# Decoder layer on one core: a share of the light feed-forward matmuls, the score reads and the heavy layer's loads and turns are moved to other places

## The chip, the cores and the metric

The kernel runs on 1 core of one Trainium2 chip, as one launch. Its metric is the device time of that launch in microseconds (us). TensorE is called PE below, VectorE DVE, ScalarE ACT, GpSimd POOL; SP is the engine that issues most DMAs.

## The reference, cut to what matters

x is (2, 2048, 512) in float32. The layer has three parts, each with a layernorm ahead and a residual sum behind it.

```python
x = x + self_attention(layernorm(x))            # 16 heads of 64, relative position bias
x = x + cross_attention(layernorm(x), context)  # 16 heads of 32, 77 masked keys
x = x + ffn(layernorm(x))
def ffn(x):
    light = gelu(rms_norm(x, gamma_l) @ w1_light + b1_light) @ w2_light + b2_light   # all rows, 256 hidden
    s = x @ routing_token
    a = 0; b = -relu(s)
    for _ in range(50):
        a = eps * log(8) - eps * logsumexp((s + b) / eps);  b = -relu(s + a)
    scores = exp((s + a + b) / eps)
    idx = top_k(scores, 512)                                  # 512 of the 2048 rows of each batch
    heavy = gelu(rms_norm(x[idx], gamma_h) @ w1_heavy + b1_heavy) @ w2_heavy + b2_heavy  # 2048 hidden
    return light + scatter(heavy * gain, idx)
```

## The kernel before, in words

The program has three stages, each in its own block; between two stages all engines meet at a barrier, and the semaphores are cleared. Every matmul that must be exact is done as three products of a high and a low float32r part (hi*hi, hi*lo, lo*hi).

**Stage 1** (`attention`) is the self-attention and takes most of the time. The change does not touch its work.

**Stage 2** (`middle`) walks over 32 tiles of 128 rows (`NTILES = 32`). It is a software pipeline of four ages: in step j, age 0 works on tile j (output projection `wo`, layernorm, turn, query projection), age 1 on tile j-1 (energies and softmax), age 2 on tile j-2 (probabilities turned, values, projection `wo2`, second residual), age 3 on tile j-3 (layernorm, rms norm `r3`, its turn into `t3_hi`/`t3_lo`, dot product with the routing token). In steps 32, 33 and 34 only the older ages are left, so less and less work stands in each. The order on each engine is written out by hand in one `iteration(j, a, here, more)` per engine. SP stores r3, t3 (a high and a low part, 256 KB each per tile), xb (the residual plus bias) and, for each 4 tiles, the scores s into DRAM scratch. At its end SP waits until all stores have landed.

**Stage 3** (`routed`) starts with SP reading the scores back (`s_in`, four small DMAs), the light layer's first weights `wl1` and the normed rows in chunks of 512 tokens (`tokens_in`, two DMAs of 1 MB for each of 8 chunks, into the two halves of `t3`). Then come the 50 routing iterations (`N_ITERS`). Each is one chain: DVE `arg` (L2029), ACT `Exp` (L1936), a PE matmul with one column (L1805), ACT `Ln` (L1939), DVE again. Behind the one-column matmul of each iteration from number 6 on PE gets four of the 192 light-layer matmuls (`hidden_mm`, L1787; one chunk is 24 of them); the 16 that are left stand behind the loop. ACT and DVE split `wl1` into high and low within iterations 3 and 4. A chunk's DMAs are issued when the chunk two before it has been multiplied.

Behind the loop the scores are spread over PSUM (L1817), the 512th largest is searched in five levels on DVE (L2072), and the chosen rows' places are turned to one-hot marks (`hot_of`, L2150) and gathered by matmuls (L1846). In all of these steps light tiles are mixed in: PE `light_mm` (L1800, four passes), then DVE `light_out` (L2022), which needs `xb[j]` from DRAM; SP issues `xb_in(j + 4)` right after it stores tile j. The last 12 tiles (`LIGHT_LAST`, 20 to 31) run beside the marks of batch 1: one mark for each of the first eight, two for each of the last four. SP also loads the heavy layer's `w2` in four DMAs of 1 MB, behind the stores of tiles 8, 12, 16 and 20 (`W2_AT`). ACT makes `w1_hi` (L1957) after the gelus; DVE makes `w1_lo` (`first_weights_low`, L2173), one piece per tile of `LIGHT_LAST`.

Then the gathered rows of batch 0 are turned (`turn_rows`, PE L1882, ACT L1968, DVE `turned_low` L2186), and the heavy layer runs: `first` (L1895) and `second` (L1911), 16 times 12 matmuls each for each of two batches, PE without a gap; last come 8 scatters on POOL.

## Time and profile before

| | us |
|---|---|
| median of 3 runs | 3987.68 (3982.39 to 3989.78) |
| the profiled execution | 3983.49 |
| its span, first to last instruction | 3981.7 |
| PE busy in the span | 3856.2 (97%) |
| end of stage 1, first instructions of stage 2 | about 2990 |
| first instruction of stage 3 | 3610.57 |
| heavy layer's first matmul | 3792.69 |

Times in the rows below are us from the start of the span. A timeline row says when an instruction (or a group of them, xN) starts and how long it takes, and in brackets how long its engine had been idle and what it waited for. "PEclk" is the granted clock of TensorE, 1.00 for 2.4 GHz and 0.50 for 1.2 GHz.

### The profile page before, as it was taken

The page shows a single profiled execution, that of the slowest core. Times are in us where ns is not written, and L with a number is a line of the kernel's source. Part 1 is how long each engine was busy: PE and PEld are TensorE (multiplying, and loading weights), DVE is VectorE, ACT ScalarE, POOL GpSimd, SP SyncE. Part 2 cuts the span into 40 slices and gives each one's busy share as a digit, 9 for nine tenths or more (in the row PEclk, how much of TensorE's full clock was granted, in tenths as well). Part 3 has the DMA queues.
Part 4 walks back from the last instruction along what each step waited for, and adds up shares of the span by engine and source line. Part 5 has one row for each costly group of instructions (what it writes and reads, how often), then busy time and mean ns, then how long its engine had stood idle before and what let it go on. Part 6 is the DMA issues. An engine that isn't in the chain of part 4 may idle for free. (4 is left out here: it accounts for less than half of the span.)

```text
span 3981.7 us, 59812 instructions
## 1 busy us (share of the span) xinstructions
PE 3856.2 (97%) x18973; PEld 2188.4 (55%) x18973; DVE 2459.3 (62%) x3356; ACT 2036.6 (51%) x3452; POOL 2687.4 (67%) x1402
## 2 busy tenths in 40 slices
PE   9999999999999999999999999999998999996899
PEld 7754444444444444444444444444446888884477
DVE  3466666666666666666666666666635777774632
ACT  3335555555555555555555555555543555543232
POOL 1128888888888888888888888888983434330010
PEclk9999999999999999999999999999998999997999
DMA  7642222322223342222322223322312333325710
GB/s 222 170 100 59 59 59 72 99 60 64 60 59 87 88 140 65 59 59 78 94 60 64 60 59 89 82 62 59 99 51 74 107 102 105 101 83 185 282 42 22
DMA packets 395504, 352.29 MB, mean 88 GB/s; under 512 B 193947, under 2 KB 268187, under 8 KB 394008
## 3 DMA queue, kind: packets, MB, share of 16 engines
q1 hardware_dynamic: 327320, 326.04, 28.5%
q10 hardware_dynamic: 66048, 16.78, 1.9%
q0 software_dynamic: 1920, 6.29, 0.5%
q8 instruction: 172, 2.82, 0.3%
q14 instruction: 44, 0.36, 0.0%
HBM read 142.64 MB, written 89.70 MB: 58 GB/s over the span
## 5 line engine op out<-in xcount | busy, mean ns | idle before, releaser
L328 POOL TENSOR_TENSOR acc<-acc,probs 128x1024 f32<-128x1024 f32 x894 | 2128.1, 2380 | 260.5 <-ACT probs L798 135.7
L928 DVE TENSOR_REDUCE maxes<-ps 128x1 f32<-128x1024 f32 x1024 | 1251.2, 1222 | 695.3 <-PE ps L579 690.7
L801 ACT ACTIVATE probs<-ps,far_bias 128x1024 f32<-128x1024 f32 (+7 forms) x1280 | 1023.0, 820 | 1012.2 <-DVE near_s L945 553.8
L614 PE MATMUL ps<-probs,v_head 128*64 128x512 f32 x4096 | 991.8, 605 | 2.0 <-ACT ctx_out L784 2.0
L579 PE MATMUL ps<-stacks 64*128 64x512 f32 x2048 | 747.2, 445 | 16.1 <-issue 7.2
L594 PE MATMUL ps<-stacks 64*128 64x512 f32 x1792 | 659.7, 447 | 0.3 <-ACT probs L798 0.3
L593 PE MATMUL ps<-stacks 128*128 128x512 f32 x2048 | 617.5, 418 | 1.7 <-ACT probs L798 1.7
L594 PEld LDWEIGHTS ps<-stacks 64*128 64x128 f32 x1792 | 275.8, 184 | 501.6 <-issue 329.8
L614 PEld LDWEIGHTS ps<-probs,v_head 128*64 128x64 f32 x4096 | 248.4, 136 | 482.9 <-issue 480.6
L593 PEld LDWEIGHTS ps<-stacks 128*128 128x128 f32 x2048 | 349.7, 188 | 217.8 <-issue 163.6
L945 DVE TENSOR_TENSOR near_s<-ps,near_bias 128x384 f32<-128x384 f32 (+2 forms) x576 | 284.8, 494 | 265.5 <-PE ps L594 243.2
L579 PEld LDWEIGHTS ps<-stacks 64*128 64x128 f32 x2048 | 302.6, 185 | 113.4 <-DVE maxes L928 57.0
L798 ACT ACTIVATE probs<-near_s 128x384 f32<-128x384 f32 (+2 forms) x576 | 271.5, 471 | 0.0
L562 PE MATMUL ps<-xn_hi,w_hi 128*128 128x512 f32 x512 | 203.8, 398 | 0.0
L562 PE MATMUL ps<-xn_hi,w_lo 128*128 128x512 f32 x512 | 203.0, 397 | 0.0
L562 PE MATMUL ps<-xn_lo,w_hi 128*128 128x512 f32 x512 | 202.8, 396 | 0.0
L325 POOL TENSOR_TENSOR acc<-probs 128x1024 f32<-128x1024 f32 x64 | 152.7, 2386 | 38.5 <-issue 31.8
L538 PE MATMUL ps<-stacks,xn_hi 128*128 128x512 f32 x512 | 165.3, 404 | 11.0 <-DVE xn_lo L898 9.0
L1251 POOL TENSOR_TENSOR m_rs<-m_rs,m_expo 128x1 f32<-128x1 f32 x32 | 17.6, 550 | 234.1 <-DVE m_rs L1456 234.1
L1361 PEld LDWEIGHTS m_ps<-m_turned,both_wk 128*128 128x128 f32 x1024 | 122.1, 196 | 4.5 <-ACT m_turned L1419 2.0
L1361 PE MATMUL m_ps<-m_turned,both_wk 128*128 128x128 f32 x1024 | 122.7, 279 | 1.4 <-ACT m_turned L1419 1.4
L1374 ACT COPY m_pt<-m_ps 77x512 f32<-77x512 f32 x128 | 68.4, 583 | 107.5 <-PE m_ps L1282 107.5
(269 smaller groups left out, 4749.3 us busy)
## 6 DMA issues: line engine op xcount, KB each, us to landing
stacks<-c_k SPq DMA_DIRECT2D x128, 256.0 KB, 2.5
stacks<-c_q SPq DMA_DIRECT2D x128, 256.0 KB, 2.6
stacks<-c_d SPq DMA_DIRECT2D x256, 128.0 KB, 2.7
scr_v<-probs ACTq DMA_DIRECT2D x32, 512.0 KB, 4.0
stacks<-c_q SPq DMA_DIRECT2D x128, 128.0 KB, 2.7
v_head<-scr_v SPq DMA_DIRECT2D x32, 512.0 KB, 3.6
scr_ctx<-ctx_out SPq DMA_DIRECT2D x128, 128.0 KB, 2.3
both_ctx<-scr_ctx SPq DMA_DIRECT2D x32, 512.0 KB, 3.9
```

The source lines that it names most:

```text
L328: pool.tensor_tensor(acc[:, qb, :], acc[:, qb, :], pr, ALU.add).then_inc(s["summed"], 1)
L538: mm = pe.matmul(ps[:, value_bank(v), :], xs[i][:, k, t * P:(t + 1) * P], (wv_hi, wv_lo)[j][:, k, half * 512:(half + 1) * 512], start=at = ...
L562: mm = pe.matmul(ps[:, proj_bank(m, tb), :], w[wi][:, kk, :], xs[xi][:, kk, tb * 512:(tb + 1) * 512], start=a == 0, stop=a == len(TERMS) - 1)
L579: mm = pe.matmul(ps[:, max_bank(n, qt, pair) + i, :], stacks[0:64, mside, QA, qt * P:(qt + 1) * P], stacks[0:64, mside, KX, kc * 512:(kc + ...
L593: return pe.matmul(out, stacks[:, side, KA, keys], stacks[:, side, QA, q], start=False, stop=True, skip_group_check=True)
L594: return pe.matmul(out, stacks[64:128, side, KX, keys], stacks[64:128, side, QB, q], start=False, stop=True, skip_group_check=True)
L614: mm = pe.matmul(ps[64 * half:64 * half + 64, PV, :], v_head[:, side, kt, :], probs[:, st % PT_RING, half * 512:(half + 1) * 512], start=k ...
L798: ins = act.activation(probs[:, st % PT_RING, a:z], near_s[:, st % 2, 0:z - a], ACT.Exp)
L801: ins = act.activation(probs[:, st % PT_RING, a:z], sc[:, a:z], ACT.Exp, bias=bias)
L928: dve.tensor_reduce(maxes[:, qt, pair:pair + 1], ps[:, bank:bank + 2, :], AX.XY, ALU.max).then_inc(s["max_done"], 1)
L945: dve.tensor_tensor(near_s[:, st % 2, 0:z - a], sc, near_bias[:, side, j0:j0 + z - a], ALU.add).then_inc(s["biased"], 1)
L1361: mm = pe.matmul(ps[:, Q2, m * P:(m + 1) * P], wq2[:, k, m * P:(m + 1) * P], turned1[:, k, :], start=k == 0, stop=k == KT - 1)
```

## The change

It moves work, and adds no arithmetic.

1. A quarter of the light layer's first matmuls (chunks 0 and 1, 48 of 192) goes into stage 2's last steps: 6 at the head of PE's step 32, 16 at the head of step 33, 14 at the head of step 34 and 12 behind the turns there. SP loads the two chunks (4 DMAs of 1 MB) at the head of its step 32; the very first of the 48 waits for chunk 0. DVE copies the results out of PSUM. `wl1` is loaded at stage 2's start and split at the end of step 30.
2. The scores are read back at the end of stage 2, two DMAs by SP and two by ACT; SP no longer waits there for the last stores, it does so at stage 3's start, ahead of chunks 2 and 3.
3. In the routing loop the light matmuls start in iteration 2, three to an iteration (144 of them), and none stands behind the loop.
4. `w2`'s four loads are issued by ACT, one behind the other, when `w1_hi` is done.
5. The turns of batch 0 (PE, ACT and DVE) go into the last four tiles of `LIGHT_LAST`, in the place of four pieces of `w1_lo`, which are made in the heavy layer's first steps.
6. Buffers are placed anew so that this fits (`keep` and `mask_i` in `e`, `hot` over the old `wl1_hi`/`wl1_lo`, r3's rows of batch 1 over the early hidden values).

```diff
@@ middle: SP @@
+            for dst, name in ((wl1, "w1l"), (gamma_l[:], "gamma_l")):
+                sp.dma_start(dst, io[name]).then_inc(s["wl1_in"], 16)
             def iteration(j, a, here, more):
                 side, other = a % 2, 1 - a % 2
+                if isinstance(j, int) and j == NTILES:
+                    sp.wait_ge(s["wo"], NTILES)
+                    for ch in range(N_EARLY):
+                        for w in range(2):
+                            sp.wait_ge(s["t3_stored"][w], 64 * (ch + 1))
+                        for part in range(2):
+                            sp.dma_start(tokens[ch][:, part, :, :].bitcast(F32),
+                                         scr["t3"][part][:, :, ch * TOKENS:(ch + 1) * TOKENS]).then_inc(s["t3_early"][ch], 16)
...
             iterations(sp, iteration)
-            for side in range(2):
-                sp.wait_ge(s["r3_stored"][side], 16 * NTILES // 2)
-                sp.wait_ge(s["xb_stored"][side], 16 * NTILES // 2)
-                sp.wait_ge(s["t3_stored"][side], 32 * NTILES // 2)
             sp.wait_ge(s["s_stored"], 16 * NBLK)
+            for half in range(2):
+                sp.dma_start(scores_of(NB - 1, half), scr_s[NB - 1, HALF * half:HALF * half + HALF]).then_inc(s["s_in"], 16)
@@ middle: PE @@
+            def light_early(first_at, end_at):
+                for n in range(first_at, end_at):
+                    q, at = divmod(n, len(HIDDEN_TERMS))
+                    ch, m = divmod(q, LM)
+                    if at == 0:
+                        if q == 0:
+                            pe.wait_ge(s["wl1_lo"], 1)
+                            pe.wait_ge(s["x1"], NTILES)
+                        if q == 1:
+                            pe.wait_ge(s["q2"], NTILES * CM)
+                        if m == 0:
+                            pe.wait_ge(s["t3_early"][ch], 32)
+                        if q >= 2:
+                            pe.wait_ge(s["hid"], q - 1)
+                    k, part, w = HIDDEN_TERMS[at]
+                    mm = pe.matmul(ps[:, (WO, Q2)[q % 2], :], (wl1_hi, wl1_lo)[w][:, k, m * P:(m + 1) * P], tokens[ch][:, part, k, :],
+                                   start=at == 0, stop=at == len(HIDDEN_TERMS) - 1)
+                    if at == len(HIDDEN_TERMS) - 1:
+                        mm.then_inc(s["hid_mm"], 1)
             def iteration(j, a, here, more):
+                if isinstance(j, int) and j in EARLY_AT:
+                    light_early(*EARLY_AT[j])
...
                     mm.then_inc(s["rt"], 1)
+                    if isinstance(j, int) and j == NTILES + 2:
+                        light_early(*EARLY_LAST)
@@ middle: ACT, at its end @@
+            act.wait_ge(s["s_stored"], 16 * NBLK)
+            for b in range(NB - 1):
+                for half in range(2):
+                    act.dma_start(scores_of(b, half), scr_s[b, HALF * half:HALF * half + HALF]).then_inc(s["s_in"], 16)
@@ constants @@
-HIDDEN_FROM, HIDDEN_STEP = 6, 4
-SPLIT_AT = 3
+N_EARLY = 2
+EARLY_AT, EARLY_LAST = {NTILES: (0, 6), NTILES + 1: (6, 22), NTILES + 2: (22, 36)}, (36, 48)
+EARLY_OUT = {NTILES + 1: (0,), NTILES + 2: (2, 3)}
+HIDDEN = [(ch, m, at) for ch in range(N_EARLY, NCHUNK) for m in range(LM) for at in range(len(HIDDEN_TERMS))]
+HIDDEN_FROM, HIDDEN_STEP = 2, 3
-G_RING, W2_AT = 3, (8, 12, 16, 20)
+G_RING = 3
+TURN_FROM = len(LIGHT_LAST) - HT
@@ routed: SP @@
-            for b in range(NB):
-                for half in range(2):
-                    s_in(b, half)
-            for dst, name in LOADS_HIDDEN:
-                sp.dma_start(dst, io[name]).then_inc(s["wl1_in"], 16)
-            for ch in range(2):
+            for side in range(2):
+                sp.wait_ge(s["t3_stored"][side], 32 * NTILES // 2)
+                sp.wait_ge(s["xb_stored"][side], 16 * NTILES // 2)
+                sp.wait_ge(s["r3_stored"][side], 16 * NTILES // 2)
+            for ch in range(N_EARLY, N_EARLY + 2):
                 tokens_in(ch)
...
-                if j in W2_AT:
-                    q = W2_AT.index(j)
-                    if q == 0:
-                        sp.wait_ge(s["hidden_mm"], NCHUNK * LM)
-                    sp.dma_start(w2[:, 4 * q:4 * q + 4, :], io["w2h"][:, 4 * q:4 * q + 4, :]).then_inc(s["w2_in"][q], 16)
@@ routed: PE, last light tiles @@
             for i, j in enumerate(LIGHT_LAST):
                 light_mm(j)
                 for t in hots_of(i):
                     hot_mm(1, t)
+                if i >= TURN_FROM:
+                    turn_rows(0, i - TURN_FROM)
@@ routed: ACT, behind w1_hi @@
+            act.wait_ge(s["hidden_mm"], N_HIDDEN_MM)
+            for q in range(4):
+                act.dma_start(w2[:, 4 * q:4 * q + 4, :], io["w2h"][:, 4 * q:4 * q + 4, :]).then_inc(s["w2_in"][q], 16)
@@ routed: DVE, last light tiles @@
                 light_out(j)
-                first_weights_low(i)
+                if i >= TURN_FROM:
+                    turned_low(0, i - TURN_FROM)
+                else:
+                    first_weights_low(i)
             pairs_out(1)
-            turned_low(0)
```

## Rows read from the trace of the kernel before

**Rows 1.** By window: us, busy time by engine, PEclk, DMA share, GB/s.

```profile
3580.00:3600.00 20.00, 9.45 (x69) 7.02 (x67) 11.47 (x20) 6.24 (x10) 3.31 (x6) 0.83 0.26 80
3650.00:3695.00 45.00, 43.18 (x191) 29.57 (x191) 22.86 (x103) 14.99 (x91) 0.00 (x0) 0.97 0.80 264
```

**Rows 2.** Timeline, stage 2's last steps: start, us, engine, line, instruction [idle before].

```profile
3570.80 0.34 SPq L1194 DMA_DIRECT2D scr_xb<-both_wo  x1
...
3572.12 1.10 PE L1282 MATMUL m_ps<-m_ident,m_e 128*77 128x128 f32 x8 [3.07 <-DVE m_e L1518]
...
3587.70 3.76 PE L1282 MATMUL m_ps<-m_ident,m_e 128*77 128x128 f32 x16 [6.72 <-DVE m_e L1518]
...
3603.14 1.12 PE L1335 MATMUL m_ps<-m_ident,m_r 128*128 128x128 f32 x4 [6.18 <-DVE m_r L1483]
...
3606.26 0.64 SPq L1191 DMA_DIRECT2D scr_t<-both_t_lo  x1
```

**Rows 3.** Timeline of stage 3's start.

```profile
3610.58 2.67 SPq L1699 DMA_DIRECT2D r_s_half<-scr_s  x4
...
3614.70 0.18 DVE L1998 TENSOR_REDUCE r_top<-r_s_half 128x1 f32<-128x32 f32 x1 [3.44 <-DMA r_s_half<-scr_s]
...
3617.19 0.24 DVE L2029 TENSOR_SCALAR r_arg<-r_ahead,r_log 128x32 f32<-128x32 f32 x1
...
3618.75 0.24 DVE L2029 TENSOR_SCALAR r_arg<-r_ahead,r_log 128x32 f32<-128x32 f32 x1 [1.31 <-ACT r_log L1939]
```

**Rows 4.** Chain that ended last, in the routing loop: start, us, what.

```profile
3629.28 1.92 PE r_ps L1787 x4
...
3631.41 1.92 PE r_ps L1787 x4
...
3640.11 8.81 DMA r_t<-scr_t
...
3692.52 1.04 PE r_ps L1787 x4
...
3693.88 1.05 PE r_ps L1787 x4
```

**Rows 5.** DMA issues of chunks 0, 1: first; second and third (us to landing).

```profile
r_t<-scr_t SPq DMA_DIRECT2D x1, 1024.0 KB, 7.8
...
r_t<-scr_t SPq DMA_DIRECT2D x2, 1024.0 KB, 11.8
```

**Rows 6.** Timeline behind the routing loop.

```profile
3695.93 0.19 DVE L2060 TENSOR_TENSOR r_score<-r_ex,r_kept 128x32 f32<-128x32 f32 x1
...
3698.76 3.71 PE L1817 MATMUL r_ps<-r_ident,r_score 128*64 128x128 f32 x64
```

**Rows 7.** Timeline: DVE sums of light tiles 20, 24, 25 and 31.

```profile
3759.88 0.69 DVE L2022 TENSOR_TENSOR r_light<-r_ps,r_xb 128x512 f32<-128x512 f32 x1 [0.77 <-PE r_ps L1800]
...
3768.06 0.69 DVE L2022 TENSOR_TENSOR r_light<-r_ps,r_xb 128x512 f32<-128x512 f32 x1 [0.44 <-PE r_ps L1800]
...
3773.22 0.69 DVE L2022 TENSOR_TENSOR r_light<-r_ps,r_xb 128x512 f32<-128x512 f32 x1 [3.41 <-DMA r_xb<-scr_xb]
...
3787.33 0.69 DVE L2022 TENSOR_TENSOR r_light<-r_ps,r_xb 128x512 f32<-128x512 f32 x1
```

**Rows 8.** Chain, heavy layer: its first group, and one further on.

```profile
3792.69 4.57 PE r_ps L1895 x12
...
3803.25 2.72 PE r_ps L1895 x12
```

**Rows 9.** Queues in 3765 to 3767 us: packets, MB, share of 16 engines.

```profile
q1 hardware_dynamic: 101, 0.53, 84.4%
q0 software_dynamic: 27, 0.07, 13.7%
```

**Rows 10.** All DMAs of xb in 3700 to 3790 us.

```profile
DMA to landing us min/median/max: 2.7/3.6/10.2
```

**Rows 11.** Timeline of ACT behind the gelus (w1_hi).

```profile
3707.02 9.91 ACT L1957 ACTIVATE r_w_hi<-r_w,r_gamma 128x512 fp32r<-128x512 f32 x16
```

More of the change, by code:

```diff
@@ L1081, with middle @@
 AGES = 4
-def middle(nc, io, scr, homes):
+def middle(nc, io, scr, homes, early):
     with ExitStack() as c:
@@ L1126, in middle @@
             ctx_hi ctx_lo mask1 zero held held_pool s_stored""".split()}
-        for n in ("ctx_in", "x_in", "xb_stored", "r3_stored", "t3_stored"):
+        for n in ("ctx_in", "x_in"):
             s[n] = (sem(n + "0"), sem(n + "1"))
+        own = dict(s)
+        s.update(early)
         block = c.enter_context(nc.Block())
@@ L1429, in iteration @@
                         act.activation(q2[:, m, :], ps[:, Q2, m * P:(m + 1) * P], ACT.Identity, bias=bq[:, m:m + 1]).then_inc(s["q2"], 1)
+                if isinstance(j, int) and j == NTILES - 2:
+                    act.wait_ge(s["wl1_in"], 32)
+                    for k in range(KT):
+                        ins = act.activation(wl1_hi[:, k, :], wl1[:, k, :], ACT.Identity, scale=gamma_l[:, k:k + 1])
+                    ins.then_inc(s["wl1_hi"], 1)
             context_hi(0, 0)
@@ L1518, in iteration @@
                     dve.tensor_tensor(et, et, sm[:].unsqueeze(2).to_broadcast([P, CH, CL]), ALU.mult).then_inc(s["p"], 1)
+                if isinstance(j, int) and j == NTILES - 2:
+                    dve.wait_ge(s["wl1_hi"], 1)
+                    for k in range(KT):
+                        ins = dve.scalar_tensor_tensor(wl1_lo[:, k, :], wl1[:, k, :], gamma_l[:, k:k + 1], wl1_hi[:, k, :].bitcast(F32), ALU.mult, ALU.subtract)
+                    ins.then_inc(s["wl1_lo"], 1)
+                if isinstance(j, int) and j in EARLY_OUT:
+                    for q in EARLY_OUT[j]:
+                        hidden_out(q)
             iterations(dve, iteration)
-    return all_of(s)
+    return all_of(own)
 HEAVY, NUM_HEAVY = 2048, 512
@@ L1553, in hidden_done @@
     last = len(HIDDEN_TERMS) - 1
-    return [ch * LM + m for ch, m, at in hidden_of(i) if at == last]
+    return [(ch - N_EARLY) * LM + m for ch, m, at in hidden_of(i) if at == last]
 LIGHT_IN_LEVEL = 2
@@ L1581, in hots_of, with routed @@
     return [i] if i < single else [2 * i - single, 2 * i - single + 1]
+N_HIDDEN_MM = (NCHUNK - N_EARLY) * LM
 HALF = P // NB
-def routed(nc, io, scr, out, index):
+def routed(nc, io, scr, out, index, homes, early):
     with ExitStack() as c:
@@ L1661, in routed @@
         HOT, TURN, FIRST, PAIRS = 7, 4, 4, (4, 7)
-        s = {n: sem(n) for n in """weights w1_in const zero s_in s_max_in top_own top_turned top_row top_wide top_mm lift scaled ahead gam dif ex mm logs neg_a neg_mm arg kept sc1 sc score w
+        s = {n: sem(n) for n in """weights w1_in const zero s_max_in top_own top_turned top_row top_wide top_mm lift scaled ahead gam dif ex mm logs neg_a neg_mm arg kept sc1 sc score w
             bc bcr t1 cnt en en_mm f1 f2 base over mm1 r1 r2 r3s sel mm2 p1 p2 place hot hot_mm pairs pairs_tr parts4 gain edge_own edge_mm edge picked index
-            tr trt trl w1_lo w2_hi w2_lo gmm g g_hi g_lo used ymm y1 y scattered light_in wl1_in wl1_hi wl1_lo hidden_mm hidden gelu_l light_mm light""".split()}
+            tr trt trl w1_lo w2_hi w2_lo gmm g g_hi g_lo used ymm y1 y scattered light_in hidden_mm hidden gelu_l light_mm light""".split()}
         for n in ("gathered", "y_in", "t3_in"):
             s[n] = (sem(n + "_0"), sem(n + "_1"))
+        s.update(early)
         for n in ("xb_in", "light_stored", "w2_in"):
@@ L1926, in _ @@
                 if b + 1 < NB:
-                    turn_rows(b + 1)
+                    for t in range(HT):
+                        turn_rows(b + 1, t)
                 second(b, HM - 1)
@@ L1939, in _ @@
                 act.activation(log[:], ps[:, 0, 0:1], ACT.Ln, scale=1.0 / K_ROUTE).then_inc(s["logs"], 1)
-                if i == SPLIT_AT:
-                    act.wait_ge(s["wl1_in"], N_HIDDEN)
-                    for k in range(KT):
-                        ins = act.activation(wl1_hi[:, k, :], wl1[:, k, :], ACT.Identity, scale=gamma_l[:, k:k + 1])
-                    ins.then_inc(s["wl1_hi"], 1)
             act.wait_ge(s["arg"], 1)
@@ L2267, in program, with handed, right @@
         clear(nc, attention(nc, io, scr, homes))
-        clear(nc, middle(nc, io, scr, homes))
-    routed(nc, io, scr, out, index)
+        early = {n: nc.alloc_semaphore("r_" + n) for n in ("s_in", "wl1_in", "wl1_hi", "wl1_lo", "hid_mm", "hid")}
+        for n in ("t3_early", "xb_stored", "r3_stored", "t3_stored"):
+            early[n] = (nc.alloc_semaphore(f"r_{n}_0"), nc.alloc_semaphore(f"r_{n}_1"))
+        clear(nc, middle(nc, io, scr, homes, early))
+    routed(nc, io, scr, out, index, homes, early)
+def handed(nc, c, stage):
+    def right(name, dims, dt=F32):
+        return c.enter_context(nc.sbuf_tensor(stage + name, dims, dt, side="right"))
+    rows_1 = right("rows_1", [P, HT, D])
+    s_half = right("s_half", [P, 2, NT])
+    hidden_0 = rows_1[:, :, :].rearrange("p (m a) d -> p m (a d)", m=LM)
+    return rows_1, s_half, hidden_0, right
 def kernel(**inputs):
```

132 lines of the change are left out of this document (68 added, 64 removed).

## The prediction, made before the run

> **What bounds the kernel now.** I read the busy times by window first: the heavy layer and stages 1 and 2 keep PE full, so only three places are left where moved work can count: stage 2's last steps, where PE works 9.45 us of 20 and the clock is down to 0.83 [rows 1], the routing loop, and the last light tiles with what follows. For each I then read the timeline (what ended the idle time) and the chain that ended last.
>
> In stage 2's last steps each step hangs on the softmax chain of the step before: PE waits 3.07, 6.72 and 6.18 us at the heads of steps 32, 33 and in 34 [rows 2]. The reader should see when SP gets to step 32: its last issue of step 31 starts at 3570.80, because it waits for xb.
>
> Stage 3's start: SP's last issue of stage 2 ends at 3606.90; stage 3 begins at 3610.5; the scores arrive at 3614.7; the routing loop starts at 3617.19 [rows 2, 3]. The first iterations take 1.56 us each, at the low clock [rows 3]. With four light matmuls an iteration takes 2.13 us at 1.2 GHz and 1.36 at 2.4 GHz [rows 4]; in the second, PE is not the bound: it idles 0.37 us of each, waiting for ACT's `Exp`, so 1.35 is the length of the ACT-DVE-PE chain and three matmuls will not shorten it. The whole loop is 76.3 us to the last one-column matmul (3693.50, just ahead of the last row of [rows 4]), against 50 x 1.35 = 67.5; the rest is low clock, the split of `wl1` (1.5) and three waits of 1.1 for chunks that take 9.4 us from issue (0.55 and 8.81 after it, [rows 4]) where PE uses one up in 8.1.
>
> The last light tiles: pace 2.05 us (8.18 for four), then 3.41 us of waiting for xb behind `w2`'s last quarter, and 5.4 us from the last tile's sum to the heavy layer, whose first 12 matmuls take 4.57 us instead of 2.72 [rows 7, 8].
>
> **Stage 2's end.** The 48 matmuls fit into the idle spells, but the first of them waits for chunk 0, and it stands ahead of all of step 32 on PE. SP can issue it only at 3571.15, after xb. When does it land? Two such loads alone took 9.4 us [rows 4]; in stage 3, four in a row landed 7.8, about 10.8, 12.8 and 14.8 us after their own issues, in order, so the second came 11.4 us after the first issue (with 0.5 MB of `wl1` ahead of it) [rows 5]. I take 10.0, so 3581.2. Bounds 9.4 and 11.4. PE then does its six at the low clock (it has idled since 3569; four take 1.92 less overhead, 0.43 each [rows 4]): 2.6 us. The turns of step 32 start at 3583.9 instead of 3572.12: 11.8 late. They and the energies run partly at 1.2 GHz: +1.3 (0.5 to 2.1; the stretch takes 4.1 us at full clock). Behind this everything queues: the energies, DVE's softmax, step 33's turns, SP's stores. Given back: step 33's 16 turns took 3.76 at the low clock; with PE kept busy ahead of them they are ACT-bound, -1.1; step 34's turns 1.12 to 0.66, -0.5. So the tail is 11.5 us late. The 16, 14 and 12 further matmuls (3.8, 3.3, 2.8 us) lie in waits of 6.7 and 6.2 us and beside SP's issues, and cost nothing; if PE were still at 1.2 GHz they would take 6.9, 6.0 and 5.2, and the last would cost about 1.5. The `wl1` split at step 30 (1.7 us on ACT and on DVE) lies under 5.9 us of `wo` matmuls: 0, at most 0.5; the same for its loads at stage 2's start.
>
> SP's two score reads (1.3 us) take the place of the wait for the last stores' landing (2.2), then the barrier (1.4): stage 3 starts at 3606.9 + 11.5 + 1.3 + 1.4 = 3621.1, 10.6 late.
>
> **Routing loop.** The scores are there at 3621.1; DVE's memsets (0.8 us) and 2.5 us of preparation remain: the loop starts at 3624.4, 7.2 late (3.4 won). Iteration 2 then needs chunk 2, issued from 3621.2 on, landed at 3631.2 by the same 10.0; its first light matmul would be ready at 3628.6, so 2.6 us are lost. From there 47 iterations to the last: three at the low clock (2.13 - 0.43 = 1.70), 44 at 1.35, sum 64.5: 3695.7, against 3693.88 [rows 4]: 1.8 late. No chunk is late any more (8 x 1.35 = 10.8 us of use against 9.4 to load). Behind the loop, the scores are ready 2.05 us after this point, but PE begins to spread them only at 3698.76, because of the 16 matmuls in front [rows 6]; now at once: 3697.9. That is 0.8 early. So parts 1 to 3, the bulk of the change, come out at -0.8.
>
> **Level search and w2.** ACT starts the gelus 1.8 late, ends `w1_hi` at 3716.93 + 1.8 = 3718.7 [rows 11], and puts 4 MB on its own queue, in the middle of the search, where SP moves about 235 GB/s of xb and out. xb is asked for four tiles (8.9 us) ahead and takes 3.6 [rows 10], so 5.3 us are spare. How do two queues share? In 3765 to 3767 us SP's queue held `w2`'s quarter (5.2 KB a packet on average, 0.53 MB / 101) and POOL's queue the row gathers (2.6 KB): 84.4% of the DMA time against 13.7% [rows 9]. If xb's queue gets 15 to 20%, `w2` takes some 13 us (3720 to 3733) and SP moves 0.07 MB/us. The pair of tiles 6 and 7 asks at 3721.4 for 1 MB (two stores, two xb); 0.8 is through by 3733, the rest by 3733.7; tile 11 wants its xb at 3728.9: a stall of 4.5 us on DVE, which holds the path. Bounds: 0 if the queues share by need, 9 if the next pair is caught as well. I take 4.5, as the row on sharing is the nearest.
>
> The Trainium skill (DMA: Bandwidth & Descriptors, Queues, rings and completion order) says that each engine goes round between the queues that have work, a whole packet at a time. By that rule 8 KB packets of `w2` against 2 KB ones of xb leave xb a fifth, and the stall is the one above; with equal shares in bytes it would be nothing. The trace's 84.4 to 13.7 agrees with the rule.
>
> **Last light tiles.** Without `w2`'s quarter in front, xb for tile 25 lands some 3 us earlier (1 MB at 340 GB/s), just in time. Tiles 25 to 31 then take 7 x 2.05 plus a second mark's 0.2 in four: 15.0 instead of 19.3, -4.3. The turns make the last four tiles longer: marks 0.9, PE's second mark 0.23 and turn 0.5, ACT's copy 0.6, DVE's low part 0.65 with hand-overs, a ring of 3.1 us in place of 2.2. From the start of these four to the heavy layer: 4 x 3.15 = 12.6 to the last low part, against 4 x 2.18 + 5.4 less the 1.3 in which the last sum stands ahead of its end = about 12.8 before. Hence about 0; with the tighter start -0.2 (bounds -2 and +3: a ring of 2.7 or 4). But PE now idles little before the first group: 4.57 becomes 2.72 [rows 8]: -1.8. The four pieces of `w1_lo` (0.74 each) go under groups of 2.72: 0; first needed at the ninth group, made by the fourth or fifth. The sum of this part: -6.3; from bounds on the stall's return (-3 to -5) and the ring: -3 to -9.
>
> **Sum.** -0.8 + 4.5 - 6.3 = -2.6 us on 3983.49, the profiled execution, which is 4.2 under the median of the runs shown. On the median: 3987.7 - 2.6 = 3985.1.
>
> **Rivals.**
> 1. *The queues share by need*: no stall in the search, -7.1 us, 3980.6. For it: SP's requests are pipelined. Against: the measured shares [rows 9].
> 2. *w2 hits more than one pair of tiles*: 4 to 5 us more, +2, 3990. For it: the stores stand in the same queue. Against: after 3733 the queue drains at some 360 GB/s.
> 3. *The wait for chunk 0 costs little*: if PE got it within the 3.07 us of idle, the tail would be 11.5 us earlier and all of that stays: 3973.6. It decides from a landing at 3572.1 on; the rows give 9.4 us at least from an issue at 3571.15. Very unlikely in full, a part (loads faster with four in flight) less so.
> 4. *Slower: the clock falls in the routing loop.* With three matmuls PE has 0.70 + 0.22 = 0.92 us of work in 1.35, and idles 0.4 to 0.6 in each iteration; with four the clock was 0.97 over the loop [rows 1]. If it stays at 1.2 GHz, 44 iterations of 1.70 add 15.4 us: 4000.5. It is slower by over 0.2% from about 30 such iterations on. Against it: in the one-hot stretch (3740 to 3756) PE has 2.4 of 3.7 us and keeps the full clock.
>
> The Trainium skill (TensorE: Matmul & The Clock Gate, A second HAM failure mode: psum-queue depth-cycling) tells of a kernel in which frequent short idle spells between groups of matmuls made the clock swing between its levels. By that rule the loop comes out as rival 4 has it; the loop with four, at 0.97, neither shows nor excludes it.
>
> **How the numbers follow.** My forecast (stall of one pair, full clock) 0.48; rival 1 0.22; rival 2 0.12; rival 3, in full or half, 0.10; rival 4, in full or half, 0.08. The range for 8 in 10 takes in rivals 1 and 2, the landing bounds (±1.5 twice), the clock's 2 us and the turns' +3: 3975 to 3995. 0.2% is 8 us, about what a measurement of this kernel can tell from no change. Faster by more: rival 3, 0.08; a third of rival 1 with its errors, 0.08; 0.05 of the main case: 0.21. Slower by more: rival 4, 0.07; a third of rival 2, 0.04; 0.05 of the main case: 0.16. Within: 0.63.
>
> **What would show it.** PE idle some 12 us until about 3581 before the first light matmul of step 32, released by a DMA; stage 3's first instruction near 3621; loop start near 3624.4, one wait of about 2.6 for chunk 2, then iterations of 1.35 and no DMA wait; PE spreading the scores near 3698; a DVE wait for xb of 4 to 5 us near tile 10 or 11 and none after tile 24; the heavy layer's first matmul near 3791.9, at full clock. It is wrong if the chunk lands much sooner or later, if the granted clock in the loop is under 0.9, or if the xb waits are absent or repeat.

## The result, and the profile after

The changed kernel takes 3992.8 us (median of 20 runs, 3987.6 to 4002.0), the one before 3986.0 (20 runs, 3981.5 to 3994.1). The ratio is 1.0015, with a 95% interval of 1.0009 to 1.0021: 6 us slower (3.6 to 8.4). That lies inside the stated range of 3975 to 3995 us, but it is a small loss where a gain of 2.6 us was forecast.

The profiled execution took 3992.33 us (span 3990.5), 8.8 more than the one before. Some of that lies ahead of everything that the change touches: DVE's first instruction of stage 2 starts at 3000.8, before at 2995.4. Over all thirteen profiles of this study it lies between 2994.5 and 3002.5, in no order with the edits, so stage 1, which the change does not touch, scatters by 8 us. The two traces are therefore laid over each other at a point inside stage 2: SP's xb store of step 31, at 3570.80 in [rows 2] and at 3576.31 now. The offset is 5.51 us, and "late" below means later by more than this offset.

The timeline of the changed kernel, stage 2's last steps to the loop's third iteration (start, us, engine, line, instruction, and in brackets the idle time before it and what ended it):

```profile
3576.31 0.34 SPq L1218 DMA_DIRECT2D scr_xb<-both_wo  x1
3576.76 1.31 SPq L1198 DMA_DIRECT2D both_wo_hi<-scr_t  x2
...
3587.56 0.76 PE L1340 MATMUL m_ps<-both_wo_hi,m_wl_hi 128*128 128x512 f32 x1 [13.00 <-DMA both_wo_hi<-scr_t]
...
3590.26 1.91 PE L1304 MATMUL m_ps<-m_ident,m_e 128*77 128x128 f32 x8
...
3607.32 3.54 PE L1304 MATMUL m_ps<-m_ident,m_e 128*77 128x128 f32 x16 [2.93 <-DVE m_e L1581]
...
3619.25 0.47 PE L1340 MATMUL m_ps<-both_wo_lo,m_wl_hi 128*128 128x512 f32 x1 [2.44 <-DVE m_rows L1505]
...
3626.29 0.64 SPq L1215 DMA_DIRECT2D scr_t<-both_t_lo  x1
...
3629.99 2.85 SPq L1773 DMA_DIRECT2D r_t<-scr_t  x4
...
3632.79 0.24 DVE L2094 TENSOR_SCALAR r_arg<-r_ahead,r_log 128x32 f32<-128x32 f32 x1
...
3640.03 0.80 PE L1847 MATMUL r_ps<-r_t,m_wl_hi 128*128 128x512 f32 x1 [2.90 <-DMA r_t<-scr_t]
```

Read it against [rows 2] and [rows 3]. PE's first light matmul (L1340) stands ahead of all of step 32 and waits 13.00 us, released by the DMA of chunk 0, which lands 10.8 us after its issue (3576.76 to 3587.56). Step 32's turns (L1304) start at 3590.26 where they started at 3572.12: 12.6 late. Step 33's turns still come after 2.93 us of idle PE. The last store of stage 2 (L1215) is issued at 3626.29 instead of 3606.26, 14.5 late. Stage 3's first instruction (3629.80, before 3610.57) is 13.7 late, and the loop (L2094) 10.1 late.

Behind the loop, the same view:

```profile
3706.59 3.71 PE L1877 MATMUL r_ps<-r_ident,r_score 128*64 128x128 f32 x64 [1.12 <-DVE r_score L2120]
...
3717.37 3.15 ACT L2017 ACTIVATE r_w_hi<-r_w,r_gamma 128x512 fp32r<-128x512 f32 x5
3719.95 0.86 ACTq L2021 DMA_DIRECT2D r_w<-in_w2h  x2
3720.43 0.71 ACT L2017 ACTIVATE r_w_hi<-r_w,r_gamma 128x512 fp32r<-128x512 f32 x1
...
3731.72 0.69 DVE L2087 TENSOR_TENSOR r_light<-r_ps,r_xb 128x512 f32<-128x512 f32 x1 [2.71 <-DMA r_xb<-scr_xb]
...
3735.54 0.69 DVE L2087 TENSOR_TENSOR r_light<-r_ps,r_xb 128x512 f32<-128x512 f32 x1 [3.13 <-DMA r_xb<-scr_xb]
...
3739.95 5.48 PE L1860 MATMUL r_ps<-r_wl,r_hidden 128*128 128x512 f32 x8
...
3803.13 0.47 PE L1956 MATMUL r_ps<-r_turned_hi,r_w_hi 128*128 128x512 f32 x1 [1.45 <-ACT r_turned_hi L2032]
```

PE spreads the scores (L1877) 2.3 late against [rows 6]. The loads of `w2` go out at 3719.95, between two pieces of `w1_hi` (L2017), not behind the last. Then DVE waits twice for xb, 2.71 and 3.13 us, for tiles 6 and 7, the two that one level of the search takes. Eight light matmuls behind that take 5.48 us where the eight at 3724.85, ahead of the waits, took 3.68. The first of the last light tiles, tile 20, is summed at 3775.67 instead of 3759.88 [rows 7], 15.79 later as the two traces stand, where the spread was 7.83 later: 7.96 us were lost since the spread. The heavy layer's first matmul starts at 3803.13 instead of 3792.69 [rows 8], 10.44 later, so 5.4 came back, and its first group of 12 takes 2.98 us instead of 4.57: 1.6 more.

Windows of the changed kernel (us, busy time by engine, PEclk, DMA share, GB/s), to compare with [rows 1]:

```profile
3660.00:3703.00 43.00, 38.01 (x161) 22.58 (x160) 22.62 (x104) 15.73 (x97) 0.00 (x0) 1.00 0.75 261
3586.00:3606.00 20.00, 16.70 (x98) 13.27 (x98) 9.46 (x12) 5.80 (x9) 2.04 (x3) 0.81 0.38 129
```

The loop runs at a granted clock of 1.00. Before it was 0.97, and all that was missing lay ahead of 3652.7; from there on it was 1.00 too. Stage 2's last steps have more PE work in 20 us, 16.70 for 9.45, and the clock is no higher for it: 0.81.

### The profile page after: what moved, and what is told of

It reads as the page before. It is cut to its first block and busy times, and to the rows that moved or that the text cites. A ratio compares the mean times of both kernels' runs of the same rounds, so it can differ in the third digit from the quotient of the medians.

```text
span 3990.5 us, 59812 instructions
## 1 busy us (share of the span) xinstructions
PE 3864.1 (97%) x18973; PEld 2188.1 (55%) x18973; DVE 2460.1 (62%) x3356; ACT 2036.5 (51%) x3452; POOL 2685.9 (67%) x1402
```

## The experiments

Eleven kernels ran, each timed in five rounds beside the kernel before on the same chip. The table gives their medians and ratios to it, and the length of each stretch in the one profiled execution, to about 0.1 us: stage 2 (from its first DVE instruction to stage 3's first), from there to the first `Exp` of the loop, from there to the score product, from there to the heavy layer's first gelu, and all from stage 2's start to the last weighed sum.

| kernel | median us | ratio, 95% interval | stage 2 | to loop | loop | to heavy | all |
|---|---|---|---|---|---|---|---|
| before | 3986.0 | 1 | 615.2 | 6.9 | 78.4 | 101.5 | 980.1 |
| after | 3992.8 | 1.0015 (1.0009 to 1.0021) | 629.1 | 3.2 | 73.2 | 99.9 | 983.6 |
| e1 early from step 33 | 3974.6 | 0.9970 (0.9958 to 0.9982) | 617.1 | 3.3 | 72.8 | 101.4 | 972.8 |
| e2 w2 on SP | 3988.0 | 1.0002 (0.9993 to 1.0011) | 629.6 | 3.3 | 74.0 | 95.3 | 980.4 |
| e3 both | 3970.8 | 0.9959 (0.9945 to 0.9972) | 613.8 | 3.3 | 74.3 | 96.0 | 965.5 |
| e4 turns last | 3992.4 | 1.0015 (1.0006 to 1.0024) | 628.1 | 3.3 | 72.8 | 100.5 | 982.8 |
| e5 w2 in the one-hot stretch | 3966.5 | 0.9945 (0.9932 to 0.9958) | 617.0 | 3.3 | 72.3 | 91.9 | 962.6 |
| e6 half of w2 in the search | 3968.8 | 0.9954 (0.9940 to 0.9967) | 618.5 | 3.2 | 72.8 | 94.7 | 967.4 |
| e7 w2 in small packets | 3974.1 | 0.9962 (0.9949 to 0.9975) | 618.2 | 3.3 | 73.0 | 95.1 | 967.7 |
| e8 before, w2 on ACT | 3992.9 | 1.0021 (1.0006 to 1.0036) | 615.9 | 6.9 | 78.2 | 101.4 | 980.6 |
| e9 no early light | 3972.7 | 0.9972 (0.9961 to 0.9984) | 615.5 | 3.3 | 77.5 | 91.9 | 966.4 |
| e10 as e5, turns last | 3967.9 | 0.9956 (0.9943 to 0.9970) | 614.8 | 3.3 | 73.0 | 92.4 | 961.6 |
| e11 before, w2 in one-hot | 3982.6 | 0.9992 (0.9983 to 1.0001) | 615.6 | 6.9 | 78.2 | 95.1 | 973.9 |

**e1: the early matmuls from step 33 on.**

```diff
-EARLY_AT, EARLY_LAST = {NTILES: (0, 6), NTILES + 1: (6, 22), NTILES + 2: (22, 36)}, (36, 48)
+EARLY_AT, EARLY_LAST = {NTILES + 1: (0, 22), NTILES + 2: (22, 36)}, (36, 48)
```

> The changed kernel with one edit: the six light matmuls ahead of step 32 are taken to step 33's head (22 there, then 14 and 12 as before). Theory (the wait for chunk 0 ahead of step 32 is what makes the end of stage 2 late, 14 us in the profile after): PE's wait of 13.0 us ahead of step 32 is gone, its 16 turns of that step start at once behind DVE's m_e, the chunk has landed before step 33's head, and stage 3 starts 12 to 14 us earlier than in the changed kernel, relative to SP's xb store of step 31. The whole is 11 to 14 us below the changed kernel, so about 3980, 6 below the kernel before. Rival (something else holds the last steps: the 48 further matmuls in them, or SP's issues): at most 4 us below the changed kernel, 3989 or more.

Measured: 3974.6, 18 us below the changed kernel (the ratios differ by 0.45%), more than the 11 to 14 expected; in the profiles stage 2 is 12.0 us shorter. The profiled execution is the slowest of the six, 3983.2 where the others lie between 3971.5 and 3976.0. The timeline of this kernel has no DMA wait on PE in these steps:

```profile
3579.35 1.99 PE L1304 MATMUL m_ps<-m_ident,m_e 128*77 128x128 f32 x8 [3.07 <-DVE m_e L1581]
...
3597.90 1.10 PE L1304 MATMUL m_ps<-m_ident,m_e 128*77 128x128 f32 x8 [1.59 <-DVE m_e L1581]
```

Step 32's turns start 1.3 us behind xb's store, as before the change, and the first eight turns of step 33 now run at full clock, 1.10 us. The wait in front of step 32 is what made the tail late; the rival falls.

**e2: w2 back on SP's queue**, behind tiles 8, 12, 16 and 20 (`W2_AT`).

```diff
-            act.wait_ge(s["hidden_mm"], N_HIDDEN_MM)
-            for q in range(4):
-                act.dma_start(w2[:, 4 * q:4 * q + 4, :], io["w2h"][:, 4 * q:4 * q + 4, :]).then_inc(s["w2_in"][q], 16)
...
+                if j in W2_AT:
+                    q = W2_AT.index(j)
...
+                    sp.dma_start(w2[:, 4 * q:4 * q + 4, :], io["w2h"][:, 4 * q:4 * q + 4, :]).then_inc(s["w2_in"][q], 16)
```

> The changed kernel with w2's four loads back on SP's queue behind tiles 8, 12, 16 and 20. Theory (the loads on ACT's queue cost 8.0 us in the level search, through late xb and the low clock behind those waits, and give 4.3 us in the last tiles): the stretch from the spread of the scores to the edge marks is 8 us shorter, the last tiles have a wait of about 3 to 4 us for xb again, the whole is 4 us below the changed kernel: 3988 to 3990. Rival (the low clock in the search comes from the light layer's having moved out of it or of the loop, not from the loads): the search stays as long, the xb wait returns, the whole is 4 us above the changed kernel, 3997.

Measured: 3988.0, 4.8 below the changed kernel. No wait for xb in the search; in the last tiles one has come back, shorter than the 3.41 of [rows 7]:

```profile
3780.03 0.69 DVE L2088 TENSOR_TENSOR r_light<-r_ps,r_xb 128x512 f32<-128x512 f32 x1 [1.95 <-DMA r_xb<-scr_xb]
```

From the sum of tile 0 to the sum of tile 11 DVE takes 21.9 us here (3716.23 to 3738.12) and 29.9 in the changed kernel (3715.61 to 3745.47): the 8.0 us are the price of `w2`'s loads there. The rival falls.

**e3: both edits.**

> Both edits of the two runs before: early matmuls from step 33 on, and w2 on SP's queue. If both theories hold they add up, since they lie in different stages: 15 to 18 us below the changed kernel, 3975 to 3978, 8 to 11 below the kernel before. If only the first holds, 3984; if only the second, 3989.

Measured: 3970.8, 22 below the changed kernel, again more than expected (15 to 18): the 18 and the 4.8 add up. Against e2, from which it differs by e1's edit, it is 17 us faster, and in the profiles stage 2 is 15.8 shorter. PE waits 1.31 us for the chunk at step 33's head, within the 6.72 us that it idled there before [rows 2], so this wait costs nothing:

```profile
3576.02 1.10 PE L1304 MATMUL m_ps<-m_ident,m_e 128*77 128x128 f32 x8 [3.07 <-DVE m_e L1581]
...
3586.19 0.47 PE L1340 MATMUL m_ps<-both_wo_hi,m_wl_hi 128*128 128x512 f32 x1 [1.31 <-DMA both_wo_hi<-scr_t]
```

In the last tiles DVE waits for xb here too, as in e2, and the heavy layer's first group runs at full clock all the same: 3.25 us from its start to the next group's, which took 4.83 before.

```profile
3765.11 0.69 DVE L2088 TENSOR_TENSOR r_light<-r_ps,r_xb 128x512 f32<-128x512 f32 x1 [2.64 <-DMA r_xb<-scr_xb]
...
3782.61 0.47 PE L1961 MATMUL r_ps<-r_turned_hi,r_w_hi 128*128 128x512 f32 x1 [1.45 <-ACT r_turned_hi L2033]
...
3785.86 0.50 PE L1961 MATMUL r_ps<-r_turned_hi,r_w_hi 128*128 128x512 f32 x1
```

**e4: the turns of the first rows behind the last light tile again**, and with them the copies and low parts.

```diff
-                if i >= TURN_FROM:
-                    turn_rows(0, i - TURN_FROM)
...
+            for t in range(HT):
+                turn_rows(0, t)
```

> The changed kernel with the turns of the first batch's rows (on PE, ACT and DVE) back behind the last light tile, and the eight pieces of w1_lo back in their places. By the sum of the prediction the move of the turns gained 0.2 us, and 1.8 more since the heavy layer's first group ran at full clock: this run is 2 us above the changed kernel, 3995. Rival (the longer ring of 3.03 us in the last four tiles cost as much as the turns did by themselves, and w2's going away made the whole gain): within 0.5 us of the changed kernel.

Measured: the same ratio as the changed kernel, and 0.4 us below it. From the first of the last four tiles' light matmuls to the heavy layer it is 13.98 us (3783.98 to 3797.96), in the changed kernel 13.47 (3789.66 to 3803.13). So the turns' move gains 0.5 us here, and not the 2 of the forecast. That group runs at full clock here as well, with the turns back where they were:

```profile
3797.96 0.47 PE L1954 MATMUL r_ps<-r_turned_hi,r_w_hi 128*128 128x512 f32 x1 [1.45 <-ACT r_turned_hi L2032]
...
3801.23 0.50 PE L1954 MATMUL r_ps<-r_turned_hi,r_w_hi 128*128 128x512 f32 x1
```

The rival is the nearer one. The turns' late place does not by itself make that group slow, 4.57 us in [rows 8]. Nor does a wait for xb of 2.64 us by itself, as e3 shows.

**e5: w2 on ACT's queue, but only in the one-hot stretch.** On top of e1:

```diff
             act.wait_ge(s["hidden_mm"], N_HIDDEN_MM)
+            act.wait_ge(s["light"], LIGHT_IN_STEP + 3)
             for q in range(4):
```

> The changed kernel with the early matmuls from step 33 on, and w2's four loads on ACT's queue, but only once tile 14 has been summed, so in the one-hot stretch, where a tile takes 3.69 us and SP's queue needs 0.5 MB in it (140 GB/s), and not amid the level search, where it needs 235. Theory (w2 costs only where both queues together ask for more than the DMA engines move): no DVE wait for xb of over 1 us anywhere; the search as short as with w2 on SP, and the wait of 1.9 to 2.6 us for xb in the last tiles, seen with w2 on SP, gone: 2 us below that kernel (3970.8), 6 below the one with w2 amid the search (3974.6): 3968 to 3970. Rival (packets of 8 KB delay those of 2 KB whatever the total): two or more waits for xb in the one-hot stretch, no gain on 3974.6.

Measured: 3966.5, the fastest kernel, 22 us below the kernel before (0.55%), 8.0 below e1 and 4.3 below e3. DVE waits for xb nowhere. But the reason in the expectation, that the two queues together ask for less than the DMA engines move, is not what the trace shows. The queues while `w2` is under way, 3728 to 3742 us (packets, MB, share of the 16 engines' time; q10 is ACT's queue, with `w2`, and q1 SP's, with xb and the stores):

```profile
q10 hardware_dynamic: 557, 4.16, 78.4%
q1 hardware_dynamic: 592, 1.08, 21.3%
```

`w2`'s queue takes most of the DMA time here as well. xb's queue moves 1.08 MB in 14 us, 77 GB/s where 140 were reckoned, and the xb of tile 19 takes 12.0 us to land (3732.09 to 3744.08), about as long as the late ones of the changed kernel (10.5 and 12.9). It is summed at 3745.73, 1.6 us later: a tile takes 3.69 us here, so xb is asked for 13.6 us ahead, where in the search it was 8. What saves this kernel is the lead, not spare room on the DMA engines.

The gain is larger than expected: part of the 4.1 us from e3 in the stretch to the heavy layer is the spread of the scores, which ran at full clock here and at half in e2 and e3 (5.38 against 3.71 us in e2).

**e6: half of w2 in the search, half in the one-hot stretch.** The added wait stands ahead of the third quarter.

> As the run before, but two of w2's quarters go where the change puts them, amid the search, and two once tile 14 has been summed: half the dose. xb is asked for some 8.9 us ahead and has about 5 us to spare. Theory (what counts is the backlog that builds up while w2 is under way, against that spare time): with 2 MB it lasts half as long, so the two waits of 2.7 and 3.1 us shrink to at most one of under 1.5 us, and the whole is within 2 us of the run before, not half way (3): 3970 to 3972. Rival (the cost goes with the bytes): half of the 6 us, 3972 to 3973, with two waits of about 1.5.

```profile
3714.41 0.69 DVE L2089 TENSOR_TENSOR r_light<-r_ps,r_xb 128x512 f32<-128x512 f32 x1 [0.45 <-DMA r_xb<-scr_xb]
...
3715.65 0.69 DVE L2089 TENSOR_TENSOR r_light<-r_ps,r_xb 128x512 f32<-128x512 f32 x1 [0.56 <-DMA r_xb<-scr_xb]
```

Measured: 3968.8, 2.2 above e5 and 5.8 below e1, and 1.0 us of waiting for half the bytes, against 6.1 for all of them in e1 (below). The cost does not go with the bytes: xb is asked for early enough to cover a short crowd. The stretch to the heavy layer, which takes in the low clock behind the waits as well, is 2.8 us longer than in e5 (94.7 against 91.9); with all of the bytes, in e1, it is 9.5 longer. In time e5 and e6 are too near for the intervals to part them; the waits part them.

**e7: w2 in the same place in packets of 2 KB.** On top of e1:

```diff
-            for q in range(4):
-                act.dma_start(w2[:, 4 * q:4 * q + 4, :], io["w2h"][:, 4 * q:4 * q + 4, :]).then_inc(s["w2_in"][q], 16)
+            for m in range(HM):
+                act.dma_start(w2[:, m:m + 1, :], io["w2h"][:, m:m + 1, :]).then_inc(s["w2_in"][m // 4], 16)
...
-                    act.wait_ge(s["w2_in"][m // 4], 16)
+                    act.wait_ge(s["w2_in"][m // 4], 64)
```

> The changed kernel with the early matmuls from step 33 on, and w2 loaded from ACT's queue in the same place, but as 16 loads whose lines are 2 KB long in place of four of 8 KB, so that its packets are no larger than those of xb. Theory (the queues take turns packet by packet, which left xb about a fifth): xb's queue now gets half, about 180 GB/s of 360 against the 235 that it asks for, the waits in the search go from 5.8 us in all to at most 1.5, and the whole is 4 to 6 us below the kernel with large packets (3974.6): about 3970. Rival (the share does not go by the packets, the sum of the bytes counts): the waits stay at 5 to 6 us and the time at 3974 to 3975.

The DMA queues (packets, MB, share of the 16 engines), while both have work: first of the changed kernel in 3726 to 3730 us, then of e7 in 3722 to 3726.

```profile
q1 hardware_dynamic: 182, 0.34, 22.0%
q10 hardware_dynamic: 181, 1.35, 79.9%
```

```profile
q1 hardware_dynamic: 445, 0.81, 52.6%
q10 hardware_dynamic: 446, 0.82, 52.9%
```

The packets are one for one in both: 182 to 181, and 445 to 446. With `w2` in packets of 7.5 KB (1.35 MB / 181) xb's queue gets 22%; with packets as large as its own it gets half. By the rule of the Trainium skill (DMA: Bandwidth & Descriptors, Queues, rings and completion order) each engine goes round between the queues that have work, a whole packet at a time, and these counts agree with it. The page lets a packet hold several descriptors, and no row here shows that, so what is shown is one for one in the packets that the profile counts. The rival that shares do not go by packets falls.

The time went less far than the share: waits of 1.09 and 1.89 us remain, 3.0 in place of e1's 6.1, and `w2` stays under way for 22.7 us in place of 15.1. About 3970 was expected, and the median is only 0.5 below e1's (the ratios differ by 0.08%, inside both intervals). In the profiles the stretch to the heavy layer is 6.3 shorter. Whether the small packets won any time in the timed runs stays open. They are no cure: each of its five runs (3970.2 to 3975.9) is slower than each of e5's (3963.3 to 3968.5).

e1's two waits, for comparison:

```profile
3721.41 0.69 DVE L2087 TENSOR_TENSOR r_light<-r_ps,r_xb 128x512 f32<-128x512 f32 x1 [2.99 <-DMA r_xb<-scr_xb]
...
3725.26 0.69 DVE L2087 TENSOR_TENSOR r_light<-r_ps,r_xb 128x512 f32<-128x512 f32 x1 [3.15 <-DMA r_xb<-scr_xb]
```

**e8: the kernel before with w2's loads on ACT's queue** behind `w1_hi`, SP's four gone, and nothing else changed.

```diff
+            act.wait_ge(s["hidden_mm"], NCHUNK * LM)
+            for q in range(4):
+                act.dma_start(w2[:, 4 * q:4 * q + 4, :], io["w2h"][:, 4 * q:4 * q + 4, :]).then_inc(s["w2_in"][q], 16)
```

> The kernel before, with one part of the change alone: w2's four loads on ACT's queue behind w1_hi. Theory (the contention belongs to this part alone): two waits for xb of about 3 us each near tiles 6 to 9 and some cold matmuls behind them, 6 to 8 us lost up to the edge marks; the last tiles win back the 3.41 us of waiting for xb behind w2's last quarter: 3 to 5 us above the kernel before, 3989 to 3991. Rival (the loss in the changed kernel needs the other parts, such as the loop with three matmuls or its shifted phase): 3 us below the kernel before, 3983.

```profile
3717.35 0.69 DVE L2021 TENSOR_TENSOR r_light<-r_ps,r_xb 128x512 f32<-128x512 f32 x1 [0.41 <-DMA r_xb<-scr_xb]
...
3724.09 0.69 DVE L2021 TENSOR_TENSOR r_light<-r_ps,r_xb 128x512 f32<-128x512 f32 x1 [2.83 <-DMA r_xb<-scr_xb]
...
3725.97 0.69 DVE L2021 TENSOR_TENSOR r_light<-r_ps,r_xb 128x512 f32<-128x512 f32 x1 [1.19 <-DMA r_xb<-scr_xb]
```

Measured: 3992.9, 5.3 above the median of before on that chip, by the ratio 8 (2 to 14). Its twelve runs lie between 3983 and 4022; without the one at 4022, 22 us above the next, the means differ by 5. The profiled one is the fastest of them, with 4.4 us of waiting for xb, and how long the others waited no trace shows. The loss needs none of the other parts: by itself this part costs about what the whole change does.

**e9: the fastest kernel without any early matmul.** `N_EARLY = 0`, and `HIDDEN_FROM, HIDDEN_STEP = 2, 4`; the copies of the early results out of PSUM are gone with them.

> The fastest kernel so far (early matmuls from step 33 on, w2 in the one-hot stretch, 3966.5) without any early matmul: all eight chunks go through the routing loop, four matmuls in each of iterations 2 to 49; the scores are still read by two queues and wl1 split in stage 2. Question: what is the early start itself worth, once PE waits for nothing because of it? Theory (the loop hangs on the chain of ACT, DVE and PE, 1.35 us an iteration with three or with four; the early start only saves waits for chunks of 1.1 us and low-clock iterations): 2 to 6 us above, 3968.5 to 3972.5. Rival (PE's 48 matmuls, 11 us at full clock, are worth their whole time): 11 us above, 3977 or more.

```profile
3642.89 0.50 PE L1845 MATMUL r_ps<-r_t,m_wl_hi 128*128 128x512 f32 x1 [1.23 <-DMA r_t<-scr_t]
...
3660.21 0.50 PE L1845 MATMUL r_ps<-r_t,m_wl_hi 128*128 128x512 f32 x1 [0.82 <-DMA r_t<-scr_t]
...
3677.07 0.50 PE L1845 MATMUL r_ps<-r_t,m_wl_hi 128*128 128x512 f32 x1 [0.71 <-DMA r_t<-scr_t]
```

Measured: 3972.7, 6.2 above e5 (by the ratios 11, with intervals of 5 us on each side). In the profiles the loop is 5.2 longer, stage 2 1.5 shorter, in all 3.8. The waits for chunks are back (1.23, 0.82, 0.71). The profiles are with the theory; the timed runs don't exclude the rival's 11. The 3.8 may itself be too small: e5's profile holds a low clock in step 32 that this one is spared (last section), and that is worth some 3 us.

**e10: the fastest kernel with the turns last.** The edit of e4 on e5.

> The same fastest kernel with the turns of the first batch's rows back behind the last light tile. The traces of the two kernels with w2 amid the search give 13.47 us from the first of the last four tiles' light matmuls to the heavy layer with the turns among them, and 13.98 with them behind, and in both the heavy layer's first group runs at full clock. So: 0.5 us above, 3967. Rival (the sum of the prediction: the turns among the tiles are what keeps the clock up for the first group, 1.8 us, and gain 0.2): 2 us above, 3968.5, with that group at 4.5 us.

Measured: 3967.9, 1.3 above e5, with intervals that overlap. The stretch to the heavy layer is 92.4 against 91.9, the 0.5 us expected, and its first group is at full clock again. Turning the rows early is worth about half a microsecond.

**e11: the kernel before with w2 in the one-hot stretch.**

> The kernel before, with w2's four loads on ACT's queue once tile 14 has been summed and nothing else changed. Theory (w2 costs nothing in the one-hot stretch, and behind it both the wait of 3.41 us for xb and the low clock of the heavy layer's first group, 4.57 against 2.72, go away since the second was the first one's doing): no DVE wait for xb over 0.5 us, and 4 to 5 us below the kernel before, 0.12% or 3982. Rival (the low clock of the first group comes from the turns behind the last tile): 3 us below, and the group stays at 4.5.

```profile
3793.35 0.47 PE L1890 MATMUL r_ps<-r_turned_hi,r_w_hi 128*128 128x512 f32 x1 [1.45 <-ACT r_turned_hi L1968]
...
3796.60 0.50 PE L1890 MATMUL r_ps<-r_turned_hi,r_w_hi 128*128 128x512 f32 x1
```

Measured: 3982.6, 2.8 below before, by the ratio 3 (7 below to 0.4 above). The timed runs are on the rival's number and can't exclude the theory's. The rows decide for the theory's mechanism: there is no wait for xb, and the first group starts at 3793.35 and the next at 3796.60, at full clock, with the turns where they always were. So the rival, that the turns' place makes that group slow, falls. The profile's stretch to the heavy layer is 6.4 shorter.

## Why the prediction was wrong

All three mechanisms of the sum were there: the wait for chunk 0, the wait for chunk 2 with a shorter loop behind it, and the crowd that `w2` makes in the search. Two terms failed. "The tail is 11.5 us late" was 14.5, because the landing took 0.8 longer and the 1.6 us that it booked as given back in steps 33 and 34 did not come back; and "I take 4.5" for the stall of the search was 8.0, because the loads met it earlier and the low clock behind the stall was not in the sum. Together they turn a gain of 2.6 into a loss of 3.3 (from xb's store of step 31 on; the timed runs say 6, and 8 us of scatter in stage 1 lie over it). The measured time stayed inside the range, which had room for errors of this size.

| step, late against before | forecast | measured |
|---|---|---|
| step 32's turns | 11.8 | 12.6 |
| last store of stage 2 ("the tail is 11.5 us late") | 11.5 | 14.5 |
| stage 3 starts | 10.6 | 13.7 |
| loop starts | 7.2 | 10.1 |
| scores spread | -0.8 | 2.3 |
| search, from the spread on | 4.5 | 8.0 |
| last light tiles to the second heavy group | -6.3 | -7.0 |
| sum | -2.6 | 3.3 |

**The stage 2 term: 11.5, measured 14.5.** The landing took 10.8, not 10.0, within the bounds: 0.8. Nearly all of the rest is what was to be given back. "With PE kept busy ahead of them" step 33's turns should have run at full clock, -1.1, but its matmuls end three microseconds before DVE's m_e, PE idles 2.93, and the turns ran at 1.2 GHz, 3.54 us for 16. With 22 matmuls there instead of 16 (e1, e3) they ran at full clock, and from xb's store of step 32 to that of step 33 it is 13.7 us there, 14.8 in the changed kernel and 15.0 before. Step 34's gift of 0.5 turned into a cost: the last 14 matmuls start at the low clock after 2.44 us of idle, and the four turns of r3 stand behind them at 3623.27, ready at 3622.5. The text had named the right condition (what if PE were still at 1.2 GHz) and priced it at 1.5, then not used it.

A question that the prediction did not ask mattered more than either term: it booked 11.8 us as the price of six matmuls and never asked what it would be worth to start them one step later. The profiles say 12 (e1) and 15.8 (e3 against e2), the timed runs 18 and 17.

**The search term: 4.5, measured 8.0.** The share was about right, 22% for 15 to 20. The rows that it was taken from did not show turns by packets, though the prediction says that they agree: in [rows 9] the packets are 101 to 27, not one for one. The changed kernel (182 to 181) and e7 (445 to 446) show them. Two things were wrong. The loads were placed behind the end of `w1_hi`, 20.8 us after the spread; they went out 13.4 after it, with eleven of the sixteen pieces of `w1_hi` still to run; no semaphore in the program makes them wait for those. So they met the requests for the xb of tiles 6 and 7 (3721.15 and 3722.56), not of 10 and 11, and both were late: 2.71 and 3.13 us, 5.84 in all. And DVE's waits left PE idle for 4.99 us, the clock was 0.50 from 3736.8 to 3743.6, and the light matmuls behind took 5.48 for 3.68: 2.1 us of the 8.0 come after the waits. Rival 2 (more than one pair of tiles hit, chance 0.12) names about this time, 4 to 5 us more where it was 3.5, but not this way: one pair was hit, both of its tiles waited, and none behind it did. That its number fits is luck.

**The loop: right.** 3.6 won ahead of it (3.4 forecast), a wait of 2.90 for chunk 2 (2.6), two slow iterations behind it of 1.71 and 1.44 us (three of 1.70), then 1.35 each, and no chunk late. Rival 4 (the clock falls with three matmuls) did not happen: the clock was 1.00. The swing of the clock that the Trainium skill tells of (TensorE: Matmul & The Clock Gate, A second HAM failure mode: psum-queue depth-cycling) does not show in this loop, though PE idles in every iteration (38.01 us busy of 43).

**The last tiles: right in sum, the cause of one part open.** -7.0 for -6.3. The -1.8 for the first group at full clock was put down to the turns' filling PE's idle time. That is not needed: e4, e8, e10 and e11 have the turns last, and the group is at full clock in all of them. But the wait for xb is not enough to slow it either: e2 and e3 wait 1.95 and 2.64 us, less than the 3.41 of before, with the turns among the tiles, and the group is at full clock. Only the kernel before has a wait and late turns together, and there the clock had come back in between. Windows of it (us, busy time by engine, PEclk, DMA share, GB/s):

```profile
3775.60:3779.00 3.40, 3.40 (x6) 1.42 (x5) 1.48 (x3) 0.00 (x0) 0.00 (x0) 0.50 0.82 284
3779.00:3792.69 13.69, 10.86 (x41) 5.07 (x40) 12.54 (x23) 2.76 (x5) 1.53 (x2) 1.00 0.33 119
3792.69:3796.10 3.41, 3.41 (x8) 2.73 (x9) 0.00 (x0) 0.00 (x0) 2.27 (x3) 0.50 0.66 192
```

The wait's own low clock is the first of these, and the group's comes 13.7 us later, behind two idle spells of 1.38 and 1.45 us around the turns. So moving `w2` alone is enough (e8, e11), and with `w2` on SP and the turns moved it is gone too (e2, e3). How the wait and the turns work together is not shown, and it hangs on one profile of the kernel before.

**The rivals 1 and 3.** Sharing by need did not happen: xb's queue got 22%. Rival 3's wait fell where the rows said it would, not cheap.

What stays open: 2 to 3 us of the timed 6 that the profiles don't place, how much the early start is worth (3.8 in the profiles, 6 to 11 in the timed runs), and what made the heavy layer's first group slow before.

## What to carry to other kernels

Work moved into an engine's idle time has to be placed after its data is there, since the first of it holds up all that stands behind it in that engine's order: six matmuls one step too early turned a gain of 0.3% into a loss of 0.15%. A load moved to another queue does not get out of the way: here the two queues took turns by packets, and the one with small packets kept a fifth, in the search and in the one-hot stretch alike. So put such a load where the other queue's data are asked for long enough ahead: 13.6 us of lead covered a landing of 12.0, and 8 us did not. Price what a stall does to the clock behind it: a quarter of the loss in the search came behind the waits, with matmuls at the low clock.

## What had not been expected of the hardware

The clock behind an idle spell is not settled by the spell. Ahead of step 32 PE does the same work in every kernel, and where no light matmul stands in front it then idles 3.07 us. Windows of 4 us from xb's store of step 31 on, in e1, e3 and e9 (us, busy time by engine, PEclk, DMA share, GB/s):

```profile
3578.03:3582.00 3.97, 2.65 (x10) 2.46 (x11) 2.43 (x5) 2.02 (x5) 0.55 (x1) 0.57 0.65 167
```

```profile
3574.70:3578.70 4.00, 2.68 (x21) 2.54 (x22) 2.43 (x5) 1.96 (x6) 0.55 (x1) 1.00 0.61 169
```

```profile
3574.31:3578.30 3.99, 2.67 (x21) 2.53 (x22) 2.43 (x5) 1.95 (x6) 0.55 (x1) 1.00 0.17 66
```

In e1, e5, e6 and e7 the granted clock is 0.53 to 0.57 there, in e10 0.81, in e3, e8, e9, e11 and before 1.00, and stage 2's step is about 3 us longer where it is low (18.4 to 18.6 against 15.6 from one xb store to the next). All the low ones load chunk 0 in this stretch, and the four kernels that don't (before, e8, e9, e11) are all at 1.00; but e3 loads it too. Whether the loads have a part in it is open. An effect of this size can't be read from one profile. It is most of the 3.3 us by which stage 2 of e1 differs from that of e3, although the two are the same kernel up to there.

A DMA that ACT issues behind activations can go out while they still run: in the changed kernel the four loads were issued between 3719.95 and 3721.3, and the last of the sixteen activations that stand ahead of them in the program ended at 3727.3.
